# Attention and spline FFN on one core: the next batch's value projections put into heads 10, 11 and 15, its first query and key units into heads 12 to 14

## What is computed

```python
q, k, v = proj(Wq, bq), proj(Wk, bk), proj(Wv, bv)          # 16 heads of 32
scores = einsum('bhqd,bhkd->bhqk', q, k) / sqrt(32) + slope(h) * (key - 511)
attn = softmax(where(causal, scores, min))
ctx = einsum('bhqk,bhkd->bhqd', attn, v)
attention = ctx @ Wo + bo
ffn = (silu(xn @ gate_w.T) * (xn @ up_w.T)) @ down_w.T      # the weights are splines of control points
```

## Time and profile before

| | |
|---|---|
| median of 3 runs | 753.85 us (752.73 to 755.12) |
| profiled execution, its own time | 753.76 us |
| its span, first to last instruction | 751.96 us (the page prints 752.0) |
| outside the span | 1.8 us |
| mean granted TensorE clock | 0.97 of full speed |
| PE busy, share of the span | 674.3 us, 90% |
| DVE, ACT, POOL busy | 463.7, 444.2 and 328.4 us |

### The profile page before, as it was taken

One profiled execution on the slowest core, in us unless ns is written; L12 is line 12 of the kernel. 1 busy time (PEld: TensorE's weight loads), 2 busy tenths in 40 slices (PEclk: granted clock), 3 DMA queues, 4 the chain that ended last, 5 costly groups with the idle time before them and its releaser, 6 DMA issues.

```text
span 752.0 us, 13688 instructions
## 1 busy us (share of the span) xinstructions
PE 674.3 (90%) x4884; PEld 541.5 (72%) x4884; DVE 463.7 (62%) x1290; ACT 444.2 (59%) x705; POOL 328.4 (44%) x191
## 2 busy tenths in 40 slices
PE   4978889989799998899898778698999999999997
PEld 3757667777578776687776666476887888888885
DVE  6277977879867879867889787587442213223212
ACT  4388777877767977777878772445443333333221
POOL 1565544554635645554646440122253236236334
PEclk9988999999899999899999899899999999999999
DMA  7888387377675473864764947974687375244001
GB/s 241 158 192 142 42 257 126 55 135 175 87 201 79 58 112 102 154 150 61 185 98 74 339 165 197 319 240 99 161 251 234 114 238 172 76 140 142 12 1 56
DMA packets 53067, 109.75 MB, mean 146 GB/s; under 512 B 6408, under 2 KB 6664, under 8 KB 51464
## 3 DMA queue, kind: packets, MB, share of 16 engines
q1 hardware_dynamic: 51416, 106.46, 58.5%
q10 hardware_dynamic: 1584, 2.43, 1.3%
HBM read 59.32 MB, written 25.17 MB: 112 GB/s over the span
## 4 chain that ended last, share of the span: by engine, by line
PE 40%; DVE 5%; POOL 5%; issue 4%; ACT 2%; DMA 2%; ACTq 1%; SPq 0%; POOLq 0%; DVEq 0%
PE bank L1516 6%; PE bank L1518 6%; PE bank L1517 6%; PE bank L1503 3%; PE bank L1504 3%; POOL resid L1684 3%; PE bank L655 3%; PE bank L600 3%; PE bank L602 2%; PE bank L601 2%; DMA taps<-windows 2%; PE bank L641 2%; POOL in_lo L1676 1%; PE bank L672 1%; PE bank L1491 1%
## 5 line engine op out<-in xcount | busy, mean ns | idle before, releaser
L1177 POOL TENSOR_TENSOR work<-work 128x1280 f16<-128x1280 f32 x64 | 171.0, 2672 | 171.2 <-ACT work L1074 171.2
L1676 POOL TENSOR_TENSOR in_lo<-inner,in_hi 128x512 fp32r<-128x512 f32 x64 | 82.6, 1293 | 197.6 <-ACT in_hi L1583 197.6
L847 DVE CUSTOM_DVE_ANT_0 work<-bank,dist 128x128 f32<-128x128 f32 (+3 forms) x256 | 115.2, 487 | 66.5 <-PE bank L641 48.2
L1066 ACT ACTIVATE work<-work,neg_max 128x128 f32<-128x128 f32 (+3 forms) x256 | 129.7, 561 | 15.3 <-DVE neg_max L847 15.1
L1633 DVE TENSOR_TENSOR inner<-bank,silu 128x512 f32<-128x512 f32 x64 | 44.1, 688 | 131.3 <-ACT silu L1577 128.6
L1583 ACT CAST in_hi<-inner 128x512 fp32r<-128x512 f32 x64 | 39.7, 620 | 134.5 <-PE bank L1518 133.6
L655 PE MATMUL bank<-ident,work 128*128 128x128 f16 x1280 | 108.3, 230 | 9.5 <-DVE work L856 6.9
L1074 ACT CAST work<-work 128x1280 f16<-128x1280 f32 x64 | 80.6, 1259 | 61.2 <-PE bank L655 60.5
L655 PEld LDWEIGHTS bank<-ident,work 128*128 128x128 f16 x1280 | 78.2, 103 | 46.0 <-issue 33.1
L1516 PE MATMUL bank<-w_room,in_hi 128*128 128x512 f32 x256 | 99.9, 390 | 0.7 <-POOL in_lo L1676 0.7
L1517 PE MATMUL bank<-w_room,in_hi 128*128 128x512 f32 x256 | 99.6, 389 | 0.0
(11 more groups left out here) (100 smaller groups left out, 1297.8 us busy)
## 6 DMA issues: line engine op xcount, KB each, us to landing
q_stack<-parts SPq DMA_DIRECT2D x48, 256.0 KB, 5.7
k_stack<-parts SPq DMA_DIRECT2D x48, 256.0 KB, 6.1
z<-xt_scratch SPq DMA_DIRECT2D x128, 88.0 KB
x_in<-x SPq DMA_DIRECT2D x32, 256.0 KB, 4.7
xt_scratch<-xt_room SPq DMA_DIRECT2D x8, 1024.0 KB, 7.3
xt_room<-xt_scratch SPq DMA_DIRECT2D x6, 1024.0 KB, 10.5
factor<-c_basis SPq DMA_DIRECT2D x5, 1024.0 KB, 11.8
taps<-windows SPq DMA_DIRECT2D x5, 1024.0 KB, 13.7
```

Of the source, the lines that this page charges most:

```text
L847: dve.tensor_tensor_reduce(probs[:, s % 2, OFF[i]:OFF[i] + n], score_bank[i % 2][:, 0:n], dist[:, S - n:S], -slope(s), 3.4e38, ALU.add, AL ...
L1066: e = act.activation(tile, tile, ACT.Exp, bias=neg_max[:, s % 2, i:i + 1], scale=-1.0)
L1177: pool.tensor_tensor(probs16[:, s % 2, 1, :], probs[:, s % 2, :], probs16[:, s % 2, 0, :], ALU.subtract).then_inc(lo_ready, 1)
L1676: pool.tensor_tensor(in_lo[k % 2][:, :], inner[:, k % 2, :], in_hi[:, k % 2, :].bitcast(F32), ALU.subtract).then_inc(il_ready, 1)
```

## The change

Before, heads 9 and 10 hold no unit, heads 11 and 13 hold two. After, head 9 alone holds none and head 15 alone holds two:

| head | before | after |
|---|---|---|
| 9 | x0 x1 | x0 x1 |
| 10 | x2 x3 | v0, x2 x3 |
| 11 | v0 q0, c1 | v1, c1 |
| 12 | k0 | q0 |
| 13 | v1 q1 | k0 |
| 14 | v2 | q1 |
| 15 | v3, c2 | v2 v3, c2 |

Head 10's unit is done in one piece at the end of the head (as `rest`), before the turns x2 and x3. On DVE every `v_take` now stands between the two pairs of `bias_and_max`; `x_low` of x0 moves ahead of the normalisation of tiles 2 and 3 in step 10; `x_low` of x2 and x3 moves from the middle of step 11 to its end.

```diff
@@ -429,8 +429,8 @@
 UNITS = {0: [("k", 1)], 1: [("q", 2)], 2: [("o", 0)], 3: [("k", 2)], 4: [("o", 1)], 5: [("o", 2)], 6: [("o", 3)],
-         7: [("q", 3)], 8: [("k", 3)], 11: [("v", 0), ("q", 0)], 12: [("k", 0)], 13: [("v", 1), ("q", 1)],
-         14: [("v", 2)], 15: [("v", 3)]}
+         7: [("q", 3)], 8: [("k", 3)], 10: [("v", 0)], 11: [("v", 1)], 12: [("q", 0)], 13: [("k", 0)], 14: [("q", 1)],
+         15: [("v", 2), ("v", 3)]}
@@ -728,7 +728,7 @@
-            early, rest = ([], units) if s == 3 else (units[:1], units[1:])
+            early, rest = ([], units) if s in (3, 10) else (units[:1], units[1:])
@@ -901,13 +901,10 @@
             for of, (kind, n) in units:
-                if kind == "v" and n > 0:
+                if kind == "v":
                     v_take(of, n)
                 elif kind == "o" and n > 0:
                     add_residual(of, n)
-            if s == 11:
-                for of, (_, n) in turns:
-                    x_low(of, n)
             if s < H:
                 bias_and_max(b, s, (2, 3))
@@ -923,13 +920,16 @@
             if turned:
                 take_turned(*turned, 2)
+            if s == 10:
+                for of, (_, n) in turns[:1]:
+                    x_low(of, n)
             if carry and s == 9:
@@
-            for of, (kind, n) in turns if s not in (3, 11) else []:
+            for of, (kind, n) in turns[1:] if s == 10 else turns if s != 3 else []:
                 (x_low if kind == "x" else ctx_low)(of, n)
@@ -937,8 +937,6 @@
-            if carry and s == 11:
-                v_take(b + 1, 0)
```

## The result

| | us |
|---|---|
| changed kernel, median of 4 runs | 770.24 (768.42 to 772.39) |
| kernel before, on the same chip | 754.49 |
| ratio | 1.0198 (95%: 1.0165 to 1.0231) |
| profiled execution, its span | 771.14, 769.3 (before: 753.76, 751.96) |

The change makes the kernel 2% slower, some 16 us. The forecast was 762.3, with a range up to 766.0: the direction is right, the size is half of what came, and the time lies outside the range.

The account below looks back on a forecast made before the run. PE was taken to set the pace in heads 11 to 15 and 0, and to wait for DVE in 9 and 10. Terms of 3.15 us per batch, 9.5 in all, less 1.0 for the clock, took 753.76 to 762.3 us (758.0 to 766.0).

Parts of the forecast that it names:

- Nothing removed, units at 2.86, heads 12 to 15: Same instruction counts; a unit takes 2.86 us; heads 12 and 14 keep one, head 13 loses one, head 15 gains one.
- the 0.15 us for POOL in each of heads 14 and 15: Heads 14 and 15: 0.15 us each for POOL's subtractions in three heads in a row; bounds nothing and 0.5 us.
- Head 11 and head 0, the waits for v_take: v1 in head 11 and k1 in head 0 each wait 1.25 us for DVE's read-out; heads of 8.19 and 6.85.
- the wait of 1.24 us is not filled, it only changes its name: Head 10: v0 waits for x_low of x0 and starts as late as x2 did; 9.14 us, +2.24.
- two turns without a wait: End of head 10: after v0 the two turns follow in 0.70 us, ending the head at 211.06.
- The term for the clock: Head 9: shorter low-clock stretches take 0.5 us off in each of two batches, -1.0 in all; bounds 0 and -2.2.
- Where head 9 lies in time: Said to be the only difference between the batches; the change shifts the second and third by 3.15 and 6.3 us.
- What is hidden, and by how much: k0's transfers before head 0: 14.75 us left, landing up to 6.9; counted as nothing, with 0 to 1 us per batch kept.
- The rival of late transfers: k0's transfers come late before head 0: +1 us a batch, 765.5 us; chance 6%.
- that rival: The clock falls at each new wait of about 1 us, low stretches slowing PE: 767 to 772 us; chance 8%.
- The waits were not taken back: Rival: other engines catch up while PE waits, heads 2, 8 and 9 idle less: 758.3 us; chance 10%.

Follow-up runs that it names:

- POOL's waits: Changed kernel with POOL waiting, ahead of its subtraction in steps 10 and 11, for DVE's normalisations: 765.29, ratio 1.0133, again 767.13, 1.0127; same edit on kernel before: 755.56, 0.9991.
- the first repeat: The changed kernel run again without any edit, beside new runs of the kernel before: 770.35 against 754.32 us, ratio 1.0207.

## Why the prediction was too low

- **Nothing removed, units at 2.86, heads 12 to 15.** Right: head 13 lost 2.85 and head 15 gained 2.87 to 2.89 where no transfer was late. Of the 0.15 us for POOL in each of heads 14 and 15, 0.23 and 0.02 came.
- **Head 11 and head 0, the waits for v_take.** Right in place, number and size: 1.08 us for 1.25, heads of 8.29 and 6.86 for 8.19 and 6.85. The run that moved the two read-outs alone took both away.
- **Head 10: "the wait of 1.24 us is not filled, it only changes its name".** Right for what stands in the changed kernel, 1.39 us for x_low. With POOL held off the head takes 8.83 to 9.31 us, 9.10 in the mean of nine, against 9.14 forecast.
- **The step that failed is in head 10's term.** It costed x_low's new place by its own duration, and counted the normalisation behind it at the 0.99 us of the earlier trace rows wherever it stood, "two turns without a wait". I had read POOL nowhere in this term, though the kernel before has POOL's subtraction start at 207.63 right behind the normalisation, and the move pushes DVE 0.6 us into it. It takes 3.32 us there. PE feels little of that in head 10, which v0 covers: 9.38 us against 8.85 with POOL held off, and 9.82 against 9.30 where `qk_low` had stopped the first tile in head 9, 0.5 us each time. The dearer place is head 9, 1.9 us when its race is lost, and the forecast had no term for that at all. Together this is 3.0 us of the median (770.16 to 767.13). The overlap of DVE and POOL was put at nothing without a reason, and the duration of 1.02 us in head 9 of the kernel before was the sign of it.
- **The term for the clock had the wrong sign, because it had the wrong mechanism.** "Where head 9 lies in time" changed no low stretch for the better: head 9 took 9.32, 9.31 and 11.24 us. The first of these lies ahead of every edit and is still 0.66 longer than in the kernel before: that is the execution's, not the change's. A head 9 of about 8.6 us stood in the first batch of the kernel before, and it came up again in the second batch of two runs and the third of another, so its place in time does not make it. The third is the race, lost in head 9 (+1.91). Together with the -1.0 counted, this is 3.6 of the 6.2 us by which the heads' sum missed. No run tells what makes a head 9 short.
- **"What is hidden, and by how much": k0's transfers.** The count of the time left was right (14.75 us forecast; PE was ready 14.88 us after head 14's start). The need was taken from a landing of at most 6.9 us with the units 8.4 and 11 us apart; now q0, k0 and q1 come 5.6 to 5.7 us apart, share the same 130 GB/s and take up to 8.7. This term was counted at nothing, and it cost 1.0 us in one batch of three (0.75 of it idle time), within the bound of 1 us per batch. The rival of late transfers was given 6% and belonged beside the forecast, not against it; its 765.5 should be 765.3 by its own sum (762.3 + 3).
- **The rivals.** In the changed kernel the clock did not fall at the new waits of 1.08 and 1.39 us: the windows of heads 10 and 11 stand at 1.00, as the earlier trace rows had suggested. It fell where two waits of about 2 us followed each other, and in two of the runs with POOL's waits at the new waits of 0.84 and 1.08 in a row, 1.5 us in one head; so that rival was near in kind, not in size. The waits were not taken back.

- **What is no part of the change.** The 2.7 us outside the carried stretches do not come back in the repeats of the same kernel (0.0 and 0.5). The largest single piece is a head of the last batch without units, 9.40 us at a clock of 0.82 in the kernel before and 10.58 at 0.68 in the changed one; the repeats of the changed kernel took 9.24 and 10.63, so it differs between executions of one kernel. The median of the kernel before itself moves by 3 us from one set of runs to the next, so the last microseconds of the miss cannot be shared out.

What stays open: what decides head 9's race in an execution (8 of 33 lost without POOL's waits, at varying places, in kernels with and without the change), what makes some heads 9 short, and why k0 is late in the second batch alone.

## What to carry to other kernels

Before an SBUF-to-SBUF instruction of DVE is shifted, look at what POOL runs in the same microsecond, not only at DVE's own queue: a shift of 0.6 us cost 2.3 us of DVE here. The same instruction at two durations in one trace (0.54 and 1.02 us here) is the sign that there is something to look for. A unit put into a gap fills it only if the reader of its bank comes in time, so move the read-outs together with the unit. And where transfers are brought closer together, take their landing times at the new spacing as longer than the old rows say.

## What the runs showed of the hardware

- DVE's normalisation of a tile (line 806, input and output in SBUF) takes 0.54 us. When its turn comes while POOL subtracts, it is held until 0.3 us after POOL's end: 2.87 us in head 10 of the changed kernel (the two tiles together 3.32), 1.02 in head 9 of the kernel before. When the tile's instruction has started before POOL, it keeps its 0.54 and POOL is the longer one: 2.76 us instead of 2.62 in head 10 of the changed kernel, and up to 2.94 where POOL starts 0.08 us behind it (head 9 of the first batch in the first repeat). x_low (line 815), whose other input lies in PSUM, takes 0.68 us beside a running POOL, where POOL starts at 207.63 and x_low at 207.67, and 0.68 without. The Trainium skill ("SBUF — State Buffer", section "Who interferes with whom") states it this way: certain DVE forms, tensor_scalar among them, can take the port pair that DVE shares with GpSimd, "Whoever issues first gets the shared pair for the whole instruction", and a DVE instruction with at most one SBUF input, outside the two-port modes, does not contend. The traces agree on both counts.
- The granted clock stayed at 1.00 through single waits of 1.08 and 1.39 us, and in the four profiles with waits of 0.70 to 0.77 and 1.08 us some 0.7 us apart (before and in head 0 of the third batch). It fell to 0.50 after waits of 0.84 and 1.08 us in the same place (0.83 and 1.08 in another run), and stayed there for at least 3 us; and for some 6 us of work after 1.84 and 2.12 us of idle time with 0.63 of work between.
- Three units' transfers of 256 KB pieces, 5.6 us apart, ran at 130 GB/s with the engines full from 240 to 252; k0's landing took 7.3 us in the median and up to 8.7, against 5.7 and 6.9 at 8.4 us.
